# Output mixing of a two-layer vision block: four groups of 32 rows, eight PSUM banks, and corrections read back in 16 transfers from two queues

## The reference, cut to what matters

```python
h = jax.nn.relu(feat @ W1 + b1)
rec = (h @ W2 + b2).reshape(NB, n, OC, LH, LW)
grid = rec.reshape(LRF, LRF, n, OC, LH, LW).transpose(2, 3, 0, 4, 1, 5)
grid = grid.reshape(n, OC, H, W)
return jnp.einsum('bohw,co->bchw', grid, out_w)
```

## Time and profile before

| | |
|---|---|
| runs | 852.76 us median of 3 (852.08 to 854.6) |
| the profiled execution | 854.39 us, of which 852.6 us is the span from the first to the last instruction |
| PE busy | 727.2 us (85% of the span) |
| DVE busy | 520.7 us (61%) |
| ScalarE (ACT) busy | 488.0 us (57%) |
| GpSimd (POOL) busy | 374.6 us (44%) |
| mean granted clock of TensorE | 0.939 |
| DMA | 31.38 MB, of which 9.37 MB written to HBM |
| output stores | 32 transfers of 256 KB, all from SP |
| read-back of the corrections | 4 transfers of 224 KB, all from SP |

### The profile page before, as it was taken

How to read it: one execution, slowest core, us unless ns; L and a number is a source line. 1 busy time by engine, 2 the same in 40 slices (tenths; PEclk the granted TensorE clock), 3 DMA queues, 4 the chain that set the end, 5 groups by cost and what they waited for, 6 DMA issues and landing times. The chain is left out here.

```text
span 852.6 us, 21573 instructions
## 1 busy us (share of the span) xinstructions
PE 727.2 (85%) x8482; PEld 387.7 (45%) x8482; DVE 520.7 (61%) x964; ACT 488.0 (57%) x986; POOL 374.6 (44%) x464
## 2 busy tenths in 40 slices
PE   3676589999999999999998569999999657749587
PEld 2454155555555555555555222333333227734254
DVE  3566156666767767776668212677777966671145
ACT  3433346777777777777775448877777206723000
POOL 4467355767776677767776520021111233300000
PEclk9999879999999999999999959999999758969989
DMA  7351000000000000000000020021111203000378
GB/s 180 81 143 35 10 2 2 2 3 3 2 3 2 2 3 2 2 3 2 3 2 2 2 50 1 25 50 52 50 50 50 68 12 90 0 1 1 55 144 281
DMA packets 15436, 31.38 MB, mean 37 GB/s; under 512 B 7208, under 2 KB 9004, under 8 KB 15340
## 3 DMA queue, kind: packets, MB, share of 16 engines
q1 hardware_dynamic: 14216, 29.61, 13.9%
q10 hardware_dynamic: 856, 0.20, 0.2%
q0 software_dynamic: 272, 0.27, 0.2%
HBM read 20.70 MB, written 9.37 MB: 35 GB/s over the span
## 5 line engine op out<-in xcount | busy, mean ns | idle before, releaser
L757 POOL TENSOR_TENSOR sc<-sc,mx 128x512 f32<-128x512 f32 x128 | 133.8, 1045 | 34.2 <-DVE mx L705 34.2
L702 DVE TENSOR_TENSOR sc<-s_ps,bias_tab 128x512 f32<-128x512 f32 x128 | 87.6, 684 | 59.2 <-PE s_ps L532 59.2
L655 ACT ACTIVATE pt<-t_ps 128x512 f32<-128x512 f32 x128 | 76.0, 594 | 52.6 <-PE t_ps L543 51.4
L1199 POOL TENSOR_TENSOR square<-xs 128x1024 f32<-128x1024 f32 x16 | 33.8, 2111 | 162.1 <-DVE xs L1101 162.1
L705 DVE TENSOR_REDUCE mx<-sc 128x8 f32<-128x512 f32 x128 | 87.8, 686 | 4.4
L1018 ACT ACTIVATE hs<-h_ps,fb1s 128x512 f32<-128x512 f32 x128 | 78.2, 689 | 17.7 <-PE h_ps L932 17.6
L543 PEld LDWEIGHTS t_ps<-consts,sc 128*128 128x128 f32 x512 | 53.7, 141 | 73.1 <-issue 45.9
L543 PE MATMUL t_ps<-consts,sc 128*128 128x128 f32 x512 | 83.9, 286 | 2.2 <-ACT pt L655 1.6
L532 PE MATMUL s_ps<-kx,qu 32*64 32x128 f32 x2048 | 71.4, 276 | 1.5 <-DVE sc L702 1.4
L932 PE MATMUL h_ps<-xs,fw 64*128 64x512 f32 x256 | 68.5, 649 | 1.0 <-ACT hs L1018 1.0
L945 PE MATMUL c_ps<-hs,fw 128*64 128x512 f32 x256 | 62.0, 604 | 0.8 <-DVE fcsq L1045 0.7
(11 more groups left out here) (190 smaller groups left out, 1402.1 us busy)
## 6 DMA issues: line engine op xcount, KB each, us to landing
raw<-in_x_dram SPq DMA_DIRECT2D x32, 256.0 KB, 4.2
xr<-in_x_dram SPq DMA_DIRECT2D x32, 256.0 KB, 3.9
out_dram<-x SPq DMA_DIRECT2D x32, 256.0 KB, 3.7
rec_scratch<-r SPq DMA_DIRECT2D x4, 224.0 KB, 4.8
xs<-rec_scratch SPq DMA_DIRECT2D x4, 224.0 KB
w<-in_L_conv_W_dram SPq DMA_DIRECT2D x1, 784.0 KB
w<-in_L_conv_W_dram SPq DMA_DIRECT2D x1, 672.0 KB
consts<-in_c_consts_dram SPq DMA_DIRECT2D x1, 400.0 KB, 3.8
```

Of the source, the lines that this page charges most:

```text
L655: act.activation(pt[a][2 * hp + j][:, :, :], t_ps[:, :, :], ACT.Exp).then_inc(s["exped"], 1)
L702: dve.tensor_tensor(sc[n % KEPT][:, :, :, :], s_ps[j][:, :, :, :], bias_tab[:, j, hp], ALU.add)\
L757: pool.tensor_tensor(v, v, mx[n % KEPT][:, :].unsqueeze(2).broadcast_to([128, 8, TOK]), ALU.subtract)\
```

## The change

`grid` becomes four slots of 1024 columns, used on four groups of partitions. Pair p = 4k + q lies in slot k on the 14 partitions from 32q on. `ow` therefore holds out_w four times, at rows 32q to 32q + 13, which takes eight loads where there were two. Each half's read-back is 16 transfers of 28 KB in place of two of 224 KB: for each image of the pair, each q and each of two slots one transfer, again on seven partitions and in runs of 256 bytes. SP issues the eight for the first image, ACT the eight for the second; ACT does so after its last work on the hidden layer.

PE mixes four pairs at a time, `mix(k)`: pair q of the four multiplies rows 32q to 32q + 13 only, four products of 256 columns, into banks 2q and 2q + 1. Before the products of pair q it waits until DVE has emptied these two banks of the previous four pairs. `mixed` is raised once, after the last of the sixteen products, and DVE waits for that before the first of its eight adds. All eight banks are used, so PE also waits until DVE has taken the network's output out of banks 4 to 7. The loops are written out. Writes of `rec`, the adds themselves and the stores are as before.

```diff
-            tail_loads += [(w1s[lo:hi, :], mlp_w1[TOP * C:INDIM]), (ow[OC * a:OC * (a + 1), lo:hi], out_w)]
+            tail_loads += [(w1s[lo:hi, :], mlp_w1[TOP * C:INDIM])]
+            tail_loads += [(ow[32 * q + OC * a:32 * q + OC * (a + 1), lo:hi], out_w) for q in range(4)]
...
-            grid = yt.rearrange("o p g n -> o p (g n)")
+            grid = xs[:, 0:4]
...
+            def spread_rec(eng, h, a):
+
+                eng.wait_ge(rec_out[h], 32)
+                rows = rec_dram[256 * a + 128 * h:256 * a + 128 * (h + 1)]
+                for q in range(4):
+                    first = 32 * q + OC * a
+                    src = rows.rearrange("(k q g) (o l) -> q o k g l", k=2, q=4, l=TOK)[q]
+                    dst = grid[first:first + OC, 2 * h:2 * h + 2].rearrange("o k (g l) -> o k g l", l=TOK)
+                    for k in range(2):
+                        eng.dma_start(dst[:, k], src[:, k]).then_inc(rec_in[h], 16)
...
-                        if i % 2 == 0:
-                            continue
-                        h = i // 2
-                        sp.wait_ge(rec_out[h], 32)
-                        for a in range(2):
-                            rows = slice(256 * a + 128 * h, 256 * a + 128 * (h + 1))
-                            sp.dma_start(grid[OC * a:OC * (a + 1), 8 * h:8 * (h + 1)]
-                                         .rearrange("o p (g l) -> o (p g) l", l=TOK),
-                                         rec_dram[rows].rearrange("r (o l) -> o r l", l=TOK)).then_inc(rec_in[h], 16)
+                        if i % 2 == 1:
+                            spread_rec(sp, i // 2, 0)
...
-                    def add(p):
+                    for p in range(PAIRS):
                         for half in range(2):
-                            dve.wait_ge(s["mixed"], 2 * p + half + 1)
+                            dve.wait_ge(s["mixed"], p // 4 + 1)
                             v = x1[:, p, COLS * half:COLS * (half + 1)]
-                            dve.tensor_tensor(v, v, psb[half][:, :], ALU.add).then_inc(s["added"], 1)
-                    add(0)
-                    add(1)
-                    with dve.Fori(1, PAIRS // 2) as i:
-                        add(2 * i)
-                        add(2 * i + 1)
+                            dve.tensor_tensor(v, v, psb[2 * (p % 4) + half][:, :], ALU.add).then_inc(s["added"], 1)
...
+                    for h in range(2):
+                        spread_rec(act, h, 1)
...
-                    def mix(p):
-                        for half in range(2):
-                            after(pe, s["added"], 2 * p - 1 + half)
-                            for y in range(2):
-                                blk = grid[:, p].rearrange("o (y x h w) -> o y h x w", y=4, x=4, h=8)[:, 2 * half + y]
-                                last = pe.matmul(psb[half][:, 256 * y:256 * (y + 1)], ow[:, :], blk,
-                                                 start=True, stop=True)
-                            last.then_inc(s["mixed"], 1)
...
+                    def mix(k):
+                        for q in range(4):
+                            after(pe, s["added"], 8 * (k - 1) + 2 * q + 2)
+                            rows = slice(32 * q, 32 * q + 2 * OC)
+                            blk = grid[rows, k].rearrange("o (y x h w) -> o y h x w", y=4, x=4, h=8)
+                            for y in range(4):
+                                last = pe.matmul(psb[2 * q + y // 2][:, 256 * (y % 2):256 * (y % 2 + 1)], ow[rows, :],
+                                                 blk[:, y], start=True, stop=True)
+                        last.then_inc(s["mixed"], 1)
+                    pe.wait_ge(s["rec"], len(ROW_TILES))
+                    for k in range(4):
+                        if k % 2 == 0:
+                            pe.wait_ge(rec_in[k // 2], 256)
+                        mix(k)
```

## The result

The changed kernel takes 860.31 us (median of 8 runs, 858.62 to 862.92); beside it the kernel before took 854.08 us (8 runs). The ratio is 1.0069, 95% interval 1.0042 to 1.0095: **slower by 0.7%**, where 841 us were forecast, and outside the range that ended at 854. The profiled execution took 862.92 us, with a span of 861.1 us and a mean granted clock of 0.917 (854.39, 852.6 and 0.939 before).

What follows compares the result with a forecast made beforehand. Bound: half 0's read-back, mixing and the last add, 54 of 852.6 us. PE starts 7.4 us earlier at 805.5, mixing takes 29.8, the tail grows to 5.4: end 840.7, 11.9 gained, forecast 841 us, range 836 to 854.

Steps and rivals of the forecast that it cites:

- so I count the first four pairs at half speed: Start of mixing: PE idle for 3.7 us, so the first four pairs take 3.8 us instead of 1.9.
- I take it for all eight: Mixing: later row groups pass earlier waiting ones for all eight passes; first four pairs 1.9 us, bounds 1.9 and 7.0.
- My sign for it: Mixing: the groups' overlap is wrong if the first sixteen products take over 5 us at full clock.
- three rounds of 7.0: Mixing after the first four pairs: each round of four pairs takes 7.0 us, where before it took 8.6.
- the last eight adds 4.9: End of mixing: eight adds by DVE take 4.92 us, 5.5 without overlap between adds.
- Rival 2: Mixing: row groups do not overlap; mixing sums to 39.1 us, end at 849 us; chance 0.26 alone.
- 7.4 us were forecast: Read-back of half 0: PE starts mixing at 805.5 in place of 812.89, 7.4 us earlier.
- my 0.58 us: Read-back: time per read issue, taken from the load of `ow`; eight are 4.6 us on each queue.
- The rates of over 100 GB/s that I asked for: Read-back: sign that DMA stays above 100 GB/s for all of half 0's reads.
- Rival 1: Read-back: reads stay at 39 and 30 GB/s, no change at 852.8 us; chance 0.15, 0.03 of it with rival 2.
- Rival 3: Stores: SP's sixteen reads push its stores out, so the kernel is slower, 858 us; chance 0.13.
- 6.7 us for 5.4: Stores after the last add: the tail grows from 4.3 to 5.4 us, at 330 GB/s.

Runs made afterwards that it cites:

- Experiments 1 to 3: Kernel before with mixing products cut to 14 rows (873.52 us), or to 64 rows (875.26 us); changed kernel with every product over all 128 rows (854.83 us).
- experiment 4: Changed kernel with the four row groups taking turns product by product and one wait for all eight banks: 849.91 us, ratio 0.9931 to the kernel before.
- experiment 3: Changed kernel with every product over all 128 rows, using four zero-padded copies of `ow`: 854.83 us, ratio 0.9999 to the kernel before.
- experiment 8: Kernel before with 16 short reads a half into the old layout, all issued by SP: 853.89 us, ratio 0.9996.
- Experiment 7: Kernel before with its two long reads a half, the second issued by ACT instead of SP: 850.19 us, ratio 0.9932.

## Why the prediction was wrong

Against the forecast span of 840.7 us the profiled execution is 20.4 us late: 0.9 by its start, 1.3 in the reads, 16.9 in mixing, 1.3 in the tail.

**The clock: "so I count the first four pairs at half speed".** This step failed. I took the return of the clock from the earlier trace rows as something that PE's work brings by itself, and left out that the change takes away 114 of 128 rows of every product. Nothing in the forecast or the rivals had a low clock for all of mixing, so the range didn't reach it. Experiments 1 to 3 show the cause: at the same order and banks, 14 or 64 rows stay at 0.50, 128 rows come back to 1.00, in the kernel before as in the changed one.

**The overlap: "I take it for all eight".** This failed too. In the earlier trace rows a group had two passes, and I stretched that to eight. My sign for it, over 5 us for the first sixteen products at full clock, was set too high: 9.4 us at the low clock are some 4.7 at the full one. What shows the failure is the count of steps, 20 in the order of the change where full overlap has eight (experiment 4). The Trainium skill, "TensorE: Matmul & The Clock Gate", Part 3, "What overlaps and what doesn't", has matmuls start and end in program order. The trace shows neither that nor my step: a group's first four passes start beside the last four of the group before it, though those stand ahead in the program, and no further ones do. Where neighbours in the program are of different groups the overlap is full. Why four passes, no more and no fewer, get past a change of group, no run tells.

The two compound. Forecast and measured, term by term: the first four pairs 3.8, now 9.4; three rounds of 7.0, now 10.8 each (817.11, 827.89, 838.73, 849.50); the last eight adds 4.9, now 4.87. Experiment 4 has 3.8 and rounds of 8.8: the order costs 5.6 + 3 x 2.0 = 11.6 us at the low clock. The remaining 3 x 1.8 = 5.3 us are between experiment 4's rounds and the 7.0 that were sized at full clock. It took both steps to make the kernel slower: without overlap but at full clock its time is that of the kernel before (experiment 3, 0.9999), with overlap at the low clock it is 0.9931 of it (experiment 4). Rival 2's sizes, without overlap but at full clock, were good: 8.7, 8.5 a round, 39.1 in all; experiment 3, which is that case, has 8.85, 8.6 and 39.5. Its price of 849 us was not: experiment 3 takes 854.83, with a tail of 6.6 us where the rival had 4.3.

**The reads.** 7.4 us were forecast and 6.1 came, but for another reason. I put the gain on short transfers that keep the fast pace of the earlier trace rows. They don't: from one queue they move 39 GB/s (experiment 8). Experiment 7 puts the gain on the second queue. And the 14.5 us that I measured it against are the longest of three profiles with the same reads (12.5 to 14.5). Issues were shorter than my 0.58 us (2.86 us for eight), the last landing longer: 5.6 us after its issue, not 2.5. The rates of over 100 GB/s that I asked for appear, but with half 1's writes in them, as many bytes as the reads, issued at 802.17. Rival 1 fell with its premise, that a second queue brings nothing (experiment 7). Rival 3 fell: SP's second eight reads were out by 811.1.

**The tail.** Mis-sized, 6.7 us for 5.4. The stores drain at some 260 to 280 GB/s, not 330, and from SP's last issue to the end it is 3.4 us (857.72 to 861.1) where I had 2.2.

**What I had right:** the adds, 0.6 us apart in runs of eight; and the wait for `rec` costs nothing: in the timeline of the changed kernel PE's pause before the first passes, 5.10 us, is ended by the DMA.

```profile
807.71 9.37 PE L1604 MATMUL bank<-xs,ow 14*128 14x256 f32 x32 [5.10 <-DMA xs<-rec_scratch]
```

## What to carry to other kernels

Before you trim zero rows from a product, look at the granted clock around it: here the padding cost no time, and what it gave was twice the clock. Where row groups are to run side by side, issue the groups in turn, not a group's whole work first, and check the overlap at the length of run that you will use. When a queue's long transfer is what is awaited, try giving half of it to another queue before you cut it into pieces.

## What was not expected of the hardware

- In these runs the granted clock goes with the rows that the products use, not only with how long PE has been busy: 55 us of unbroken passes at 14 or 64 rows stay at 0.50, while 128 rows are at 1.00 from 811.6 (experiment 3). Between 64 and 128 rows nothing was tried. Products of 64 rows are no bar by themselves: in the kernel before, the stretch of the feed-forward layer has many (L932), at a clock of 1.00 throughout. But eight passes of 512 columns take 1.99 us there, where one takes 0.43 us in the earlier trace rows, so they run two at a time, and products of 128 rows (L945) stand between. A stretch of that kernel, then its timeline on PE:

```profile
560.00:620.00 60.00, 60.00 (x414) 20.59 (x410) 43.29 (x84) 45.92 (x68) 12.68 (x6) 1.00 0.17 45
```

```profile
599.32 1.99 PE L932 MATMUL h_ps<-xs,fw 64*128 64x512 f32 x8
...
601.57 0.65 PE L945 MATMUL c_ps<-hs,fw 128*64 128x512 f32 x2
```

- Two queues, each with one read of 896 runs of 256 bytes onto seven partitions, took 8.8 us from issue to first use; one queue with both took 12.5 to 14.5. Each queue kept to some 39 GB/s, alone or beside the other.
- Groups of rows overlap fully in turn (32 passes in 3.8 us) and by four passes a change when one group's eight passes come in a row (9.4 us).
